# A four-block attention network whose last stage is a 127-step recurrence: the recurrent product, the filler and the final product as strips of 32 columns

## What is computed

```python
U = (xn @ W_in.T + b_in) @ Bmat                       # (batch, T, 64)

def step(s, u_t):
    s = jax.nn.silu(s @ A.T) + u_t                    # s: (batch, 64), A: (64, 64)
    return (s, s)
_, states = jax.lax.scan(step, jnp.zeros((batch, 64)), U.transpose(1, 0, 2))
ssm_out = jnp.einsum('tbs,sh->bth', states, Cmat)     # Cmat: (64, 128)
x = residual + ssm_out
mod = program_probs.mean(axis=1) @ W_prog.T + b_prog
return x + mod[:, None, :]
```

## Time and profile before

| what | us |
|---|---|
| median of 3 runs (2118.9 to 2124.22) | 2123.61 |
| the profiled execution, its own time | 2124.64 |
| its span, first to last instruction | 2122.9 |
| mean granted TensorE clock in it, as a share of full speed | 0.978 |
| the scan, from its first weight load (2031.30) to the end of the last SiLU (2118.67) | 87.4 |

### The profile page before, as it was taken

How to read it: one execution, slowest core, us unless ns; L and a number is a source line. 1 busy time by engine, 2 the same in 40 slices (tenths; PEclk the granted TensorE clock), 3 DMA queues, 4 the chain that set the end, 5 groups by cost and what they waited for, 6 DMA issues and landing times.

```text
span 2122.9 us, 36204 instructions
## 1 busy us (share of the span) xinstructions
PE 1872.6 (88%) x13625; PEld 1198.0 (56%) x13625; DVE 1339.7 (63%) x3612; ACT 1109.4 (52%) x3858; POOL 239.0 (11%) x263
## 2 busy tenths in 40 slices
PE   5887998899988998899988998899988998877699
PEld 2555565646655565546655565556655566544345
DVE  3554768577775768577775768577775768554410
ACT  3452845557363845557363845567473836433222
POOL 0001011010212011010212011010202011010000
PEclk9999999999999999999999999999999999988999
DMA  6000000000000000000000000000000000000001
GB/s 196 1 1 6 12 1 1 1 17 2 1 1 6 12 2 1 1 17 1 1 1 6 13 1 1 1 17 2 1 2 6 1 1 1 1 1 1 1 16 25
DMA packets 25138, 20.14 MB, mean 9 GB/s; under 512 B 2243, under 2 KB 22790, under 8 KB 24966
## 3 DMA queue, kind: packets, MB, share of 16 engines
q1 hardware_dynamic: 24966, 17.83, 2.9%
HBM read 15.73 MB, written 2.10 MB: 8 GB/s over the span
## 4 chain that ended last, share of the span: by engine, by line
PE 54%; DVE 23%; ACT 17%; issue 4%; POOL 2%; SPq 1%; DMA 0%; POOLq 0%; DVEq 0%; ACTq 0%
PE ps L825 12%; PE ps L833 11%; ACT probs L1474 7%; PE ps L873 5%; ACT s_probs L1474 4%; PE ps L974 3%; PE ps L897 3%; DVE neg_max L1735 3%; DVE tok L1755 3%; DVE stats L1742 3%; PE ps L883 2%; PE ps L998 2%; PE ps L1422 2%; PE ps L869 2%; PE ps L821 2%
## 5 line engine op out<-in xcount | busy, mean ns | idle before, releaser
L1474 ACT ACTIVATE probs<-ps,neg_max 128x128 f32<-128x128 f32 x1024 | 362.2, 395 | 147.7 <-DVE neg_max L1735 146.5
L1474 ACT ACTIVATION_READ_ACCUMULATOR probs<-ps,neg_max 128x1 f32 x1024 | 238.8, 234 | 0.0
L1474 ACT ACTIVATE s_probs<-ps,s_max 128x128 f32<-128x128 f32 x672 | 183.7, 396 | 95.6 <-DVE s_max L1735 95.6
L1735 DVE TENSOR_REDUCE neg_max<-ps 128x4 f32<-128x512 f32 x256 | 164.5, 684 | 89.8 <-PE ps L873 89.8
L647 POOL TENSOR_TENSOR rstd<-var_eps,minus_half 128x4 f32<-128x4 f32 x88 | 94.4, 1072 | 1068.0 <-DVE var_eps L1748 1067.2
L1742 DVE BATCH_NORM_STATS2 stats<-ps 128x6 f32<-128x128 f32 x352 | 78.2, 284 | 181.4 <-PE ps L833 179.6
L1777 DVE TENSOR_TENSOR probs<-probs,inv 128x512 f32<-128x512 f32 x256 | 177.1, 692 | 8.8
L1468 ACT ACTIVATE probsT<-ps 128x512 f32<-128x512 f32 (+1 forms) x270 | 164.2, 629 | 27.3 <-PE ps L883 13.6
L883 PE MATMUL ps<-ident,probs 128*128 128x128 f32 x1024 | 156.5, 281 | 8.6 <-ACT queries L1468 4.6
L873 PEld LDWEIGHTS ps<-keys,queries 64*128 64x128 f32 x2048 | 125.7, 189 | 54.7 <-issue 54.7
L873 PE MATMUL ps<-keys,queries 64*128 64x128 f32 x2048 | 150.5, 287 | 0.0
(11 more groups left out here) (296 smaller groups left out, 3421.8 us busy)
## 6 DMA issues: line engine op xcount, KB each, us to landing
x_in<-in_x SPq DMA_DIRECT2D x8, 256.0 KB, 3.0
c_in<-in_ctx SPq DMA_DIRECT2D x8, 256.0 KB, 3.2
skip_in<-in_mask_BxS_ik SPq DMA_DIRECT2D x8, 256.0 KB, 3.1
out<-headsT SPq DMA_DIRECT2D x28, 64.0 KB, 1.8
valid_in<-in_mask_BxS_bf SPq DMA_DIRECT2D x8, 64.0 KB, 3.7
w_qkv_sa<-in_L_xattn_sa_wq SPq DMA_DIRECT2D x1, 512.0 KB
w_qkv_sa<-in_L_xattn_sa_wk SPq DMA_DIRECT2D x1, 512.0 KB
w_qkv_sa<-in_L_xattn_sa_wv SPq DMA_DIRECT2D x1, 512.0 KB
```

The source lines that it names most:

```text
L1474: last = A(dst[:, u % dst.shape[1], h * 128:h * 128 + 128], bank(st, (tag, "s", u))[:, h * 128:h * 128 + 128], ACT.Exp, bias=src_max[:, u ...
L1735: V.tensor_reduce(dst[:, u % 2, :], bank(st, (tag, "s", u)).rearrange("p (h k) -> p h k", h=4), AX.X, ALU.max, negate=True).then_inc(max_r ...
```

## The change

The stationary operand of all TensorE work in the scan becomes 32 columns wide, so each instruction uses one strip of 32 columns of the array (and writes the 32 PSUM partitions that belong to it).

- `scan_step`: the 64 useful columns of A as two products, on strip 0 and strip 1; `scan_mm` is raised by the second. The 64 columns of zeros are no longer loaded.
- `final_step(k - 1)` in every step: token t alone, on strip t % 4; the product with `w_c`, then the residual as a plain f32 product with `ident` instead of a transpose. It writes the same places of banks 2 and 3 as before.
- `keep_strip` in every step: 512 columns past a 32-column piece of the bf16 identity, on strip 3, or on strip 2 when strip 3 has the final product.

```diff
-            aT = turned[:, TURN["L3_xattn_A", 0], :]
+            aT = turned[:, TURN["L3_xattn_A", 0], 0:NS]
+
+            def keep_strip(strip):
+
+                mm(ps[32 * strip:32 * strip + 32, 5, :], ident_h[:, 0:32], ident_h[:, :].unsqueeze(1).broadcast_to([128, 4, 128]),
+                   start=True, stop=True)
...
-                mm(ps[:, k % 2, 0:B], aT, scan_in[:, k - 1, :], start=True, stop=True).then_inc(scan_mm, 1)
...
+                for n in range(0, NS, 32):
+                    last = mm(ps[n:n + 32, k % 2, 0:B], aT[:, n:n + 32], scan_in[:, k - 1, :], start=True, stop=True)
+                last.then_inc(scan_mm, 1)
...
-                mm(dst, final_rows(scan_in, j), w_c[:, :], start=True, stop=False)
...
-                last = mm(dst, final_rows(x2_all, j), ident[:, :], start=False, stop=True, is_transpose=True)
...
+                return n, ps[32 * strip:32 * strip + 32, 2 + n % 2, at:at + E]
...
+                mm(dst, scan_in[:, t, :], w_c[:, :], start=True, stop=False)
+                last = mm(dst, x2_all[:, t, :], ident[:, :], start=False, stop=True)
...
                 scan_step(k)
-                if k >= FINAL_STEPS and k % FINAL_STEPS == 0:
-                    final_states(k // FINAL_STEPS - 1)
-                elif k >= FINAL_STEPS and k % FINAL_STEPS == 1:
-                    final_residual(k // FINAL_STEPS - 1)
-                    keep_busy(2, 5)
-                else:
-                    keep_busy(3, 5)
+                final_step(k - 1)
+                keep_strip(2 if k % FINAL_STEPS == 0 else 3)
             pe.wait_ge(scan_silu, T - 1)
-            final_states(FINAL_BLOCKS - 1)
-            final_residual(FINAL_BLOCKS - 1)
+            final_step(T - 1)
```

More of the change, by code:

```diff
@@ L1421, in scan_step, with final_bank, final_step @@
                     pe.wait_ge(scan_silu, k - 1)
-                mm(ps[:, k % 2, 0:B], aT, scan_in[:, k - 1, :], start=True, stop=True).then_inc(scan_mm, 1)
-            def final_rows(x, j):
-                return x[:, j * FINAL_STEPS:(j + 1) * FINAL_STEPS, :].rearrange("p t b -> p (t b)")
-            def final_bank(j):
+                for n in range(0, NS, 32):
+                    last = mm(ps[n:n + 32, k % 2, 0:B], aT[:, n:n + 32], scan_in[:, k - 1, :], start=True, stop=True)
+                last.then_inc(scan_mm, 1)
+            def final_bank(t):
+                j, strip = t // FINAL_STEPS, t % FINAL_STEPS
                 n = max(n for n, (first, _) in enumerate(FINAL_GROUPS) if first <= j)
                 at = (j - FINAL_GROUPS[n][0]) * E
[L1431 to L1435, removed]
+                return n, ps[32 * strip:32 * strip + 32, 2 + n % 2, at:at + E]
+            def final_step(t):
+                n, dst = final_bank(t)
+                if t == FINAL_STEPS * FINAL_GROUPS[n][0] and n >= 2:
                     pe.wait_ge(fin_copy, n - 1)
-                mm(dst, final_rows(scan_in, j), w_c[:, :], start=True, stop=False)
-            def final_residual(j):
-                n, dst = final_bank(j)
-                last = mm(dst, final_rows(x2_all, j), ident[:, :], start=False, stop=True, is_transpose=True)
-                if j == sum(FINAL_GROUPS[n]) - 1:
+                mm(dst, scan_in[:, t, :], w_c[:, :], start=True, stop=False)
+                last = mm(dst, x2_all[:, t, :], ident[:, :], start=False, stop=True)
+                if t == FINAL_STEPS * sum(FINAL_GROUPS[n]) - 1:
                     last.then_inc(fin_mm, 1)
```

## The result

The changed kernel takes 2107.51 us (median of 4 runs, 2106.63 to 2109.66) against 2122.12 us of the kernel before (4 runs in all by then). The ratio is 0.9934, with a 95% interval of 0.9917 to 0.9951. When both ran again on one chip it is 2105.71 (5 runs) against 2124.87 us (10 runs), ratio 0.9909 (0.9896 to 0.9921). So it is faster, by 15 to 19 us; 2108.0 was forecast.

What follows compares the result with a forecast made beforehand. The scan was taken as bound by one chain of 127 links of 0.69 us. 2124.64 - 15.6 (scan) + 0.03 (tail) = 2109.1, less 1.03 to the runs' median, gave 2108.0 us; range 2104 to 2118, about 0.85.

Steps and rivals of the forecast that it cites:

- One chain of 127 links: In the scan, recurrent load and multiply, SiLU and back wait for each other: 0.69 us a link, whatever fills it.
- The recurrent product as two strips: In each scan link the product ends at 0.287 instead of 0.41 us; new link 0.565, gain 15.6 us in all.
- the burst: Head products on 32-column strips at 2006.96, ahead of the scan: sixteen matmuls in 0.64 us, read as strips running side by side.
- the bound of 0.16: Upper bound on a link's gain if both recurrent strips ran wholly beside each other: 20.3 us in all.
- What fills a link: Filler, final product and residual fit beside the chain in each scan link, so they were costed at nothing.
- The cover of 0.065: Slack per link, in us, before the final product on strip 0 or 1 delays the next recurrent product.
- Rival 1: TensorE's clock falls to 0.50 inside the scan, losing 38 us if for all of it; chance 0.12.
- Rival 2: Streams of different strips exclude each other, 2132.5 us, or only a second strip's loads wait, 2121 us; chance 0.06.
- Rival 3: Strips 0 and 1 are late for the recurrent product, links 0.60 to 0.65, 2112 to 2119 us; chance 0.08.
- The sum: Whole kernel: 2124.64 - 15.6 + 0.03 = 2109.1 for the profiled execution, 1.03 above the median, so 2108.0 us.

Runs made afterwards that it cites:

- e5: The changed kernel without the filler in the scan: 2106.43 us (4 runs), ratio to the kernel before 0.9914.
- e6: The changed kernel without the filler and without the residual's product, so the output lacks the residual: 2104.66 us (one execution).
- e2: The kernel before with only the recurrent product as two strips of 32 columns, all else 128 wide: 2117.73 us (5 runs), ratio 0.9965.
- e4: The changed kernel with only the recurrent product back at full width (128 columns): 2159.33 us (one execution), scan 112.5 us.
- e7: The changed kernel with the filler on the same strip as the final product of its link: 2116.05 us (one execution), scan 76.5 us.
- e10: The changed kernel with each link's filler issued just ahead of the recurrent product: 2127.67 us (one execution), links 0.703 us.
- e8: The kernel before without its filler in the scan: 2152.75 us (one execution), scan 114.6 us.
- e9: The kernel before with the recurrent product as two strips, the rest at full width, and no filler in the scan: 2131.66 us (one execution).
- e1: The changed kernel again, unchanged, in five rounds against the kernel before: 19.2 us faster by the medians, scan 68.7 us.
- e3: The kernel before with the recurrent product as one product of 64 columns instead of 128: 2125.74 us (one execution), scan 84.5 us.

## Why the prediction was right, and where it was not

**One chain of 127 links.** Right. The SiLU and the way back kept their times, 0.190 and 0.05 to the next load. From the product's end to the SiLU it is 0.047 by the records instead of 0.036, which no run explains; the rest of the change is the product's own part.

**The recurrent product as two strips.** The mechanism was right and the size low. The term was put at 0.123 a link, 15.6 us; it measured 0.143, 18.0 us over the 126 links between the SiLUs. What was mis-sized is the spacing of the loads. I carried 0.03 between the first load and the next over from the burst and had strip 1's first load at 0.036, its last matmul from 0.095 and its end at 0.287. In the link after, strip 1's first load starts 0.01 after strip 0's, all four matmuls start within 0.06, and the product ends at 0.26. The product alone thus gained 0.153, close to the bound of 0.16 for both strips wholly side by side; 0.011 of it went into the later SiLU.

**What fills a link, at nothing.** Right for this kernel: the link is 0.545 with the filler, without it (e5) and without the residual's product too (e6). But the prediction did not give the condition. Final product and filler start 0.09 into the link and disturb nothing only as long as they are as narrow as the recurrent product. In e2, where they are wide, a link is 0.08 longer on average than in the changed kernel; in e4, where the recurrent product is wide, it is 0.35 longer, of which 0.14 are the wide product itself (0.688 against 0.545) and 0.20 the mix. I had taken the narrow filler for a detail. The Trainium skill has the rule, "TensorEngine Tiling (Array Packing)", section "Key Properties": changing the tiling mode drains the engine, going to another tile of the same mode does not. The traces of e2 and e4 agree, with 0.09 us from the end of a stream to the next load at each change.

**The cover of 0.065 on strips 0 and 1.** Not contradicted, since all four links of the changed kernel are alike (0.545 or 0.546), but stated for the wrong resource. By e7 and e10 also strips 2 and 3 can hold up the SiLU, because completion is signalled in program order. In the changed kernel both limits are met: the final product of the link before ends about 0.69 after that link's first load, the recurrent product it precedes at 0.80.

**Rival 1, the clock.** It did not happen, 1.00 throughout. In e5 and e6, where TensorE does still less in a link, no fall came either. That the clock can fall in this scan, and what that costs, is shown by two other kernels, e8 and e9, whose plain links have nothing but the recurrent product. That the final product in each link kept the clock up after the change is argued from these four: no run leaves it out altogether.

**Rival 2, strips take turns.** Refuted by the trace after. The filler and the final product start beside each other at 2041.54. The rule of the Trainium skill cited in the prediction ("TensorE: Matmul & The Clock Gate", section "What overlaps and what doesn't") said that matmuls never pass each other and that a load overlaps only on other row groups. The traces decide against it: e7 shows starts out of program order on different column strips, and the trace after has loads beside running matmuls on the same rows (four loads in 0.14 while the first matmul, 0.217 long, runs). What the same place says of the ends, that they keep program order, agrees with e10.

**Rival 3** did not happen either; all links are alike.

**The sum.** 2108.0 against 2107.51 is closer than its terms, and that is luck. The scan gave 2.4 us more than forecast, and the part ahead of the scan, which the prediction held still, happened to be 3.1 us longer in the profiled execution. The median that the forecast started from, 2123.61, was 2122.12 with a fourth run and 2124.87 in ten others. The sentence that the time before 2031 should be unchanged to a microsecond was wrong: by the same program it moves by several us from run to run. The medians of e1 (19.2 us) and the scan's 18.0 agree with each other better than the first comparison does with either.

## What to carry to other kernels

Where a small f32 product stands in a latency chain, load only the columns it needs and put each 32 of them on a strip of its own; but then make everything that TensorE does beside it 32 columns wide too, or each change of width costs 0.09 us, as it did here. Issue what the next engine waits for ahead of filler and side work, since a matmul's signal waits for all matmuls before it, on whatever strip. Before narrowing or removing a filler, look at what else streams in each link: here the kernel with the final product in every link did without its filler (e5), and the kernel before lost its clock without it (e8).

## What the runs showed of the hardware

- A change between strips of 32 columns and the full 128, either way, holds the next weight load for about 0.09 us from the end of the last stream, an estimate from the records of e2 and e4.
- Matmuls on different column strips start out of program order (e7: strip 1 at 2060.34, strip 0, issued earlier, at 2060.53), and signal their completion in order (e10: a product over at 0.26 of the link is signalled only after a filler that was issued ahead of it, 0.39 long).
- The record of one f32 load is 0.108, 0.134 and 0.188 us for 32, 64 and 128 columns (e1, e3).
- The granted clock stayed at 1.00 in a scan whose links have the recurrent strips and two more f32 strip matmuls of 128 columns (e6). It fell to 0.50 2 and 3 us into scans whose plain links have the recurrent product alone (e8 at 2033.1, e9 at 2038.6).
- With the same program ahead of it, the scan began anywhere within 13 us over twelve traces.
